# Second layer norm and weight splits moved into the first cycle of a delta-rule layer, with key norm and inverse turns re-placed between its scores

## The chip, the cores and the metric

The kernel runs on one core of a Trainium2 chip. The metric is the device time of one execution in microseconds (us). Engines: PE is TensorE (PEld its weight loads), DVE VectorE, ACT ScalarE, POOL GpSimd, SP the queue that issues the DMAs here. Each takes its own instructions in order and waits on semaphores.

## The reference

A small vision model of two blocks on 64 images of 38 tokens (2432 tokens of width D = 256): patch embedding, softmax attention, a mixture of experts, then the block that matters here, and a feed-forward layer with ternary weights. That block's attention, for 16 heads of 16:

```python
h = h + L1_attn(_layernorm(h))          # the "second layer norm" and the "delta layer"
# inside L1_attn
q = silu(x @ Wq); k = l2norm(silu(x @ Wk)); v = silu(x @ Wv)
log_f = log_sigmoid(x @ Wf); gamma = -sigmoid(x @ Wgamma)
a = k * gamma[..., None] * exp(gk)      # gk = log_f, per head
# per token: Sp = S * exp(gk); u = a.Sp + v; S = Sp + k u; o = q.S
out = out * sigmoid(x @ Wg1 @ Wg2)
out = layernorm(out) * norm_w
return out @ Wo
```

## The kernel before

Products run in float32r: each operand is split into a high part (ScalarE copies and rounds) and a low part (the difference), and three products are summed (`split_products`). XH and XL hold the normalised, transposed activations in these two parts, in 19 tiles of 128 tokens; the delta layer takes them in 8 chunks of 304 tokens (8 images).

**Stage of the second layer norm** (`layer_norm_turn`, called from `last_layer`), closed by a barrier of all engines (line 70) on both sides. DVE normalises a tile of the residual into one of four buffers `normed_tiles` (L138), PE transposes it with two matmuls into one of four PSUM banks (L169), ACT copies it to `x_hi` (L151), DVE writes `x_lo` (L128). SP loads the weights meanwhile, in 22 transfers (L105). Before tile 9 DVE waits for all of them and then prepares some weights (L1321 to L1326); ACT and POOL split five weights (L160, L115).

**Delta layer** (`delta_layer`): a pipeline over the 8 chunks in one function `part(c, nxt, z, y)` for each engine, whose calls are cycles k = 0, 1, ... 9. In cycle k, `nxt` = k is projected to queries and keys, `c` = k-1 gets its values, decays and scores, `z` = k-2 has the inverse of its 19x19 triangular systems computed row by row on DVE (`inverse_row`, L2367 multiplies and L2370 sums), and `y` = k-3 yields outputs. Cycle 0 has only `nxt` and the low-rank gate (`low_part` on PE, L2045; `low_high` on ACT, L2248; `gate_parts` on DVE, L2470); cycles 3 to 7 have all four. The order inside a cycle is the order of calls at the end of `part`, written by hand.

The end of a cycle on PE: `output` (L2141), then scores in four rounds (`score(p)`, L2034, all into the same four PSUM banks), decays (L2011), the transposed inverse in three batches of its rows (`inverse_out`, L2078, batches in `T_BATCHES`), then the next cycle's `a_rows` (L2055, L2061) and values (L1998). `score(p)` waits until DVE has weighed round p-1 (`weigh`, L2430). DVE between these: `whole_out` (L2451), `low_out` (L2459), `inverse_row(17)` and `(18)`, `bounded` (L2411) and `unit_key` (L2417). `key_norm` (L1982) sums the squares of the keys for `bounded`. POOL makes the next decay operands (`steps`, L2567), each after the decay matmul two before it.

Of the kernel before, what the change touches and what calls it, by code (L numbers as in the profile page):

```python
# [25 lines left out]
P = 128  # L26
# [57 lines left out]


def layer_norm_turn(nc, bank, RES, STD, MV, XN, XH, XL, ident, name, loads=(), splits=(),
                    prepare=None, pool_first=None, pool_work=None):

    xh = XH[:, :, 0:TOKENS]
    xl = XL[:, :, 0:TOKENS]
    first = TILES - len(splits) - 5
    with stage(nc, name + "_var", name + "_std", name + "_inv", name + "_normed", name + "_turned",
               name + "_hi", name + "_lo", name + "_loaded", name + "_prepared",
               name + "_w_hi", name + "_w_lo") as (
            block, var_ready, std_ready, inv_ready, normed, turned, hi_ready, lo_ready,
            loaded, prepared, w_hi, w_lo):  # L100
        if loads:
            @block.sync
            def _(sp):
                for dst, src in loads:
                    sp.dma_start(dst, src).then_inc(loaded, 16)  # L105
                sp.wait_ge(loaded, 16 * len(loads))

        if splits or pool_work:
            @block.gpsimd
            def _(pool):  # L110
                if pool_first:
                    pool_first(w_lo)
                for n, (raw, hi, lo) in enumerate(splits):
                    pool.wait_ge(w_hi, n + 1)
                    nc.gpsimd.tensor_tensor(lo, raw, hi.bitcast(F32), ALU.subtract).then_inc(w_lo, 1)  # L115
                if pool_work:
                    pool_work(pool, w_lo)

        @block.vector
        def _(dve):  # L120
            nc.vector.tensor_scalar(STD[:, 0, :], MV[:, :, 1], EPS, None, ALU.add).then_inc(var_ready, 1)
            dve.wait_ge(std_ready, 1)
            nc.vector.reciprocal(STD[:, 2, :], STD[:, 1, :]).then_inc(inv_ready, 1)
            dve.wait_ge(inv_ready, 1)

            def low_part(t):
                dve.wait_ge(hi_ready, t + 1)
                nc.vector.tensor_tensor(  # L128
                    xl[:, :, t * P:(t + 1) * P], bank[t % 4][:, 0:D].rearrange("p (m t) -> p m t", m=HALVES),
                    xh[:, :, t * P:(t + 1) * P].bitcast(F32), ALU.subtract).then_inc(lo_ready, 1)  # L130

            for t in range(TILES):
                if prepare and t == first - 1:
                    dve.wait_ge(loaded, 16 * len(loads))
                    prepare[0](prepared)
                if t >= 4:
                    dve.wait_ge(turned, t - 3)
                nc.vector.tensor_scalar(XN[:, t % 4, :], RES[:, t, :], MV[:, t, 0:1], STD[:, 2, t:t + 1],  # L138
                                        ALU.subtract, ALU.mult).then_inc(normed, 1)
                if t >= 2:  # L140
                    low_part(t - 2)
            low_part(TILES - 2)
            low_part(TILES - 1)

        @block.scalar
        def _(act):
            act.wait_ge(var_ready, 1)
            nc.scalar.activation(STD[:, 1, :], STD[:, 0, :], ACT.Sqrt).then_inc(std_ready, 1)
            for t in range(TILES):
                act.wait_ge(turned, t + 1)  # L150
                nc.scalar.activation(xh[:, :, t * P:(t + 1) * P],  # L151
                                     bank[t % 4][:, 0:D].rearrange("p (m t) -> p m t", m=HALVES),
                                     ACT.Copy).then_inc(hi_ready, 1)
                if t == first and splits:
                    act.wait_ge(loaded, 16 * len(loads))
                    if prepare:
                        act.wait_ge(prepared, prepare[1])
                if 0 <= t - first < len(splits):
                    raw, hi, lo = splits[t - first]
                    nc.scalar.activation(hi, raw, ACT.Copy).then_inc(w_hi, 1)  # L160

        @block.tensor
        def _(pe):
            for t in range(TILES):
                pe.wait_ge(normed, t + 1)
                if t >= 4:
                    pe.wait_ge(lo_ready, t - 3)
                for m in range(HALVES):
                    turn = nc.tensor.transpose(bank[t % 4][:, m * P:(m + 1) * P],  # L169
                                               XN[:, t % 4, m * P:(m + 1) * P], ident[:, :])  # L170
                turn.then_inc(turned, 1)
# [1114 lines left out]
def last_layer(nc, sb, psum, bank, ins, RES, BN, MV, STD, XN, XH, XL, xh_c, xl_c, ident, identb, hmask, out):  # L1286
# [9 lines left out]
    with ExitStack() as ctx:  # L1296
# [17 lines left out]
        with ExitStack() as raw:  # L1314
# [4 lines left out]
            def norm_into_output(scaled):  # L1319
                for m in range(HALVES):  # L1320
                    nc.vector.tensor_scalar(w[:, 4, m, :], w[:, 4, m, :], nw[:, m:m + 1], None,  # L1321
                                            ALU.mult).then_inc(scaled, 1)
# [1466 lines left out]
```

## Time and profile before

| what | value |
|---|---|
| median of 3 runs | 1803.45 us (1800.07 to 1805.45) |
| profiled execution, its own time | 1798.41 us |
| its span, first to last instruction | 1796.6 us |
| granted TensorE clock, mean | 0.89 |
| busy: PE, PEld, DVE, ACT, POOL | 1644.3, 1473.5, 1102.7, 682.4, 333.2 us |
| second layer norm (window of the trace) | 1172.85 to 1196.12 us |
| cycle 0 of the delta layer | 1196.74 to 1212.68 us |
| cycles 1 to 9 | 1212.68 to 1624.4 us |

Busy shares are means over stages with different limits: most of PE's time is the mixture of experts, up to 1172 us, which the change doesn't touch. Each stage is to be read from its own windows and from the wait that ends last in it.

### The profile page before, as it was taken

To read this page: it belongs to the slowest core of one execution; us is meant where nothing else is said; L and a number is where in the kernel's file an instruction comes from. 1 tells how busy PE (TensorE), PEld (TensorE's weight loads), DVE (VectorE), ACT (ScalarE), POOL (GpSimd) and SP (SyncE) were. 2 spreads that over 40 slices of the span, in tenths; PEclk is the share of its full clock that TensorE was granted. 3 is DMA by queue.
4 is the path that set the end of the run, shared out by engine and by line. 5 is a ranking of instruction groups with operands and counts; after the bars stand their busy time and mean duration, and the time that the engine had idled before them with its cause. 6 is when DMAs were issued, how large, how long until landed. Compare 5 with 4: busy or idle time off the path is not lost. (4 is left out here: it accounts for less than half of the span.)

```text
span 1796.6 us, 49076 instructions
## 1 busy us (share of the span) xinstructions
PE 1644.3 (92%) x21601; PEld 1473.5 (82%) x21601; DVE 1102.7 (61%) x2417; ACT 682.4 (38%) x1433; POOL 333.2 (19%) x331
## 2 busy tenths in 40 slices
PE   8899968999999999999999999967889889778789
PEld 8788856898888999999999999936888778767668
DVE  7677757555455554645555455565666675665885
ACT  6466644232122232322222232245343444324642
POOL 4633336000000000000000000044232222210840
PEclk9999969999999999999999999968676665665889
DMA  6000011000000000100001000010000000001001
GB/s 216 1 2 3 3 50 48 1 25 24 1 24 24 25 24 1 48 1 24 24 3 46 1 1 1 1 38 2 3 3 4 4 4 3 4 4 53 1 12 45
DMA packets 11702, 36.10 MB, mean 20 GB/s; under 512 B 3401, under 2 KB 8033, under 8 KB 8929
## 3 DMA queue, kind: packets, MB, share of 16 engines
q1 hardware_dynamic: 11488, 32.97, 5.3%
q8 instruction: 170, 2.79, 0.6%
q14 instruction: 44, 0.35, 0.1%
HBM read 30.47 MB, written 2.49 MB: 18 GB/s over the span
## 5 line engine op out<-in xcount | busy, mean ns | idle before, releaser
L1126 ACT ACTIVATE hidden<-bank,moe_b 128x512 f32<-128x512 f32 (+1 forms) x320 | 213.3, 668 | 536.8 <-PE bank L1018 522.5
L1035 PE MATMUL bank<-moe_w2h,hidden_hi 128*128 128x256 f32 x1216 | 345.7, 284 | 0.0
L1035 PE MATMUL bank<-moe_w2l,hidden_hi 128*128 128x256 f32 x1216 | 344.0, 283 | 0.0
L1035 PE MATMUL bank<-moe_w2h,hidden_lo 128*128 128x256 f32 x1216 | 343.9, 283 | 0.0
L1160 DVE SCALAR_TENSOR_TENSOR residual<-bank,gates,residual 128x256 f32<-128x256 f32 x152 | 73.4, 483 | 290.5 <-PE bank L1035 290.5
L1018 PE MATMUL bank<-x_hi,moe_w1h 128*128 128x512 f32 (+1 forms) x640 | 243.8, 381 | 2.9 <-ACT hidden L1126 2.8
L1018 PE MATMUL bank<-x_lo,moe_w1h 128*128 128x512 f32 (+1 forms) x640 | 242.5, 379 | 0.0
L1018 PE MATMUL bank<-x_hi,moe_w1l 128*128 128x512 f32 (+1 forms) x640 | 242.1, 378 | 0.0
L1035 PEld LDWEIGHTS bank<-moe_w2h,hidden_hi 128*128 128x128 f32 x1216 | 233.0, 192 | 5.9 <-DVE residual L1160 4.3
L1035 PEld LDWEIGHTS bank<-moe_w2l,hidden_hi 128*128 128x128 f32 x1216 | 233.2, 192 | 1.2
L1035 PEld LDWEIGHTS bank<-moe_w2h,hidden_lo 128*128 128x128 f32 x1216 | 233.2, 192 | 0.0
L1148 DVE TENSOR_TENSOR hidden_lo<-hidden,hidden_hi 128x512 fp32r<-128x512 f32 (+1 forms) x320 | 215.2, 672 | 11.0
L1146 DVE CAST hidden_hi<-hidden 128x512 fp32r<-128x512 f32 (+1 forms) x320 | 133.1, 416 | 87.1 <-ACT hidden L1126 79.5
L1335 POOL MEMSET gate_low<- 80x2432 f32 x1 | 2.1, 2121 | 867.0 <-POOLq L70 867.0
L1018 PEld LDWEIGHTS bank<-x_hi,moe_w1h 128*128 128x128 f32 x640 | 120.2, 188 | 25.9 <-ACT hidden L1126 5.0
L1018 PEld LDWEIGHTS bank<-x_hi,moe_w1l 128*128 128x128 f32 x640 | 120.1, 188 | 20.4
L1018 PEld LDWEIGHTS bank<-x_lo,moe_w1h 128*128 128x128 f32 x640 | 120.3, 188 | 18.7
L2567 POOL TENSOR_TENSOR decay_steps<-log_f_parts,from_here 128x608 fp32r<-128x608 f32 x64 | 78.9, 1244 | 212.4 <-PE bank L2011 126.9
L2367 DVE TENSOR_TENSOR normed_tiles<-a_rows,inverse 128x2 f32<-128x2 f32 (+5 forms) x144 | 68.9, 479 | 3.4
L2370 DVE TENSOR_REDUCE inverse<-normed_tiles 128x2 f32<-128x2 f32 (+5 forms) x144 | 57.4, 399 | 5.0
L2034 PE MATMUL bank<-q_and_k,dk_in_pair 32*64 32x76 f32 x2048 | 35.8, 275 | 25.1 <-DVE qk_and_ak L2430 24.6
L2430 DVE TENSOR_TENSOR qk_and_ak<-bank,decay 128x304 f32<-128x304 f32 x128 | 51.5, 463 | 10.2 <-PE bank L2034 5.4
(331 smaller groups left out, 3231.2 us busy)
## 6 DMA issues: line engine op xcount, KB each, us to landing
moe_w<-in_moe_w SPq DMA_DIRECT2D x16, 1024.0 KB, 4.8
patches<-in_patches SPq DMA_DIRECT2D x7, 864.0 KB, 6.6
out<-residual SPq DMA_DIRECT2D x19, 128.0 KB, 1.7
ffn_w<-in_ffn_w SPq DMA_DIRECT2D x2, 1024.0 KB, 6.3
att_w<-in_att_w SPq DMA_DIRECT2D x1, 1536.0 KB, 9.7
delta_w<-in_delta_w SPq DMA_DIRECT2D x1, 1280.0 KB
patches<-in_patches SPq DMA_DIRECT2D x6, 144.0 KB, 2.6
tok_w<-in_tok_w SPq DMA_DIRECT2D x6, 128.0 KB, 2.4
```

The source lines that it names most:

```text
L1018: mm = nc.tensor.matmul(bank[i % 4][:, 0:n], left, right, start=(j == 0), stop=(j == len(passes) - 1))
L1035: mm = nc.tensor.matmul(bank[4 + n % 3][:, 0:D], left, right, start=(i == 0), stop=(i == len(passes) - 1))
L1126: nc.scalar.activation(H[:, i % 4, 0:n], bank[i % 4][:, 0:n], ACT.Relu, bias=b1[:, x, f:f + 1]).then_inc(acted, 1)
L1146: nc.vector.tensor_copy(HH[:, k % 2, f, 0:n], H[:, i % 4, 0:n]).then_inc(h_hi, 1)
L1148: nc.vector.tensor_tensor(HL[:, k % 2, f, 0:n], H[:, i % 4, 0:n], HH[:, k % 2, f, 0:n].bitcast(F32), ALU.subtract).then_inc(h_lo, 1)
L1160: nc.vector.scalar_tensor_tensor(out=RES[:, t, :], in0=bank[4 + n % 3][:, 0:D], scalar=G[:, t, x:x + 1], in1=RES[:, t, :], op0=ALU.mult, o ...
L1335: nc.gpsimd.memset(G1[:].bitcast(F32), 0.0).then_inc(done, 1)
L2034: mm = nc.tensor.matmul(psum[half(s), g, ts], KX[rows, m, 2 * p + s, e, :], buffers["QK"][c % 2][rows, m, 2 * p + s].rearrange("p x t -> p ...
L2367: nc.vector.tensor_tensor(PD[:, :, 0:t, 0:t], spread(AS[:, :, t, 0:t], 2, t), TT[:, :, 0:t, 0:t], ALU.mult).then_inc(t_mult, 1)
L2370: nc.vector.tensor_reduce(TT[:, :, 0:t, t], PD[:, :, 0:t, 0:t], AX.X, ALU.add).then_inc(t_solved, 1)
L2430: nc.vector.tensor_tensor(PA[c % 2][:, p, m * HPH:(m + 1) * HPH].rearrange("p (g e) x t -> p e g x t", e=2)[:, e], psum[:, 0:PPH, n * 2 * ...
L2567: nc.gpsimd.tensor_tensor(MS[:, b % 2], spread(LF[:, :, b // 2, heads].bitcast(F32), 3, SEQ), spread(spread(here[:, :], 1, HPH), 1, 2), AL ...
```

## The change

The stage `layer_norm_turn` is gone. Its work becomes the `first` branch of `part` in cycle 0, interleaved with the projections, and its raw weights lie in the buffer `qk_and_ak1`, which the first cycles leave unused. The weights of Q and K are loaded by a transfer of their own, the others by 22 more. The normalisation is now `x * inv + (-mean * inv)`: even tiles on DVE, odd tiles on ACT. The low-rank product alternates between two banks. The memsets of POOL move behind the computed statistics. One `ACT_TABLE_LOAD` and one barrier fall away. Separately, in every cycle: `decay(3)` goes ahead of `score(0)`, `key_norm(1)` from before `decay(2)` to before `score(2)`, `inverse_row(17)` ahead of the first `weigh`, `inverse_row(18)` behind the third round's; the batches of inverse rows are 8, 3 and 8 where they were 8, 8 and 3.

```diff
-T_BATCHES = (range(0, 8), range(8, 16), range(16, HALF))
+T_BATCHES = (range(0, 8), range(8, 11), range(11, HALF))
 # PE, cycle 0 (project waits for x_lo of 3 tiles and for its weights' low part)
+                if first:
+                    turns(*range(8))
+                    project(0)
+                    turns(8, 9)
+                    project(1)
+                    turns(10, 11)
+                    low_part(0)
+                    project(2)
+                    turns(12, 13)
+                    low_part(1)
+                    project(3)
+                    turns(14, 15)
+                    low_part(2)
+                    turns(16, 17, 18)
+                    key_norm(0)
+                    low_part(3)
+                    key_norm(1)
+                    low_part(4)
+                    return
 # PE, every cycle, from output on
                 output(1)
-                key_norm(1)
                 decay(2)
+                decay(3)
                 score(0)
-                decay(3)
                 inverse_out(0)
                 score(1)
                 decay(4)
                 decay(5)
+                key_norm(1)
                 score(2)
                 decay(6)
                 decay(7)
+                inverse_out(1)
                 score(3)
-                inverse_out(1)
                 inverse_out(2)
 # DVE, cycle 0, its start
+                    norm(0)
+                    norm(2)
+                    low(0)
+                    for t in (4, 6, 8):
+                        norm(t)
+                        low(t - 3, t - 2)
+                    prepare()                  # waits for all 22 transfers
+                    silu_of(0)
+                    norm(10)
+                    low(7, 8)
...
+                    low(15, 16, 17, 18)
+                    bounded(0)
+                    gate_part(2)
+                    bounded(1)
+                    decay_masks()
+                    unit_key(0)
+                    unit_key(1)
+                    gate_part(3)
+                    gate_part(4)
+                    gate_weights()
 # POOL, cycle 0
+                    pool.wait_ge(inv_ready, 2)
                     nc.gpsimd.memset(after[:].bitcast(F32), 0.0).then_inc(zeroed, 1)
...
+                    low(0)                     # low part of the K weights, then of Q
+                    low(1)
+                    nc.gpsimd.memset(G1[:].bitcast(F32), 0.0).then_inc(gate_zero, 1)
+                    nc.gpsimd.memset(wg2s[:].bitcast(F32), 0.0).then_inc(gate_zero, 1)
+                    low(2)
+                    square(0)
+                    low(3)
+                    square(1)
```

On ScalarE, the first stretch before, from the start of the layer norm's stage (`std` is the standard deviation, `x_hi` the high part, `delta_wgh` and the next ones the high parts of weights):

```order
L148 ACT_TABLE_LOAD
L148 ACTIVATE std<-std 128x19
L151 ACTIVATE x_hi<-bank 128x2x128 x10
L160 ACTIVATE delta_wgh<-delta_wg_90 128x32
L151 ACTIVATE x_hi<-bank 128x2x128
L160 ACTIVATE delta_wvfh<-delta_wvf 128x576
L151 ACTIVATE x_hi<-bank 128x2x128
L160 ACTIVATE delta_wh<-delta_w 128x512
```

And on ScalarE in cycle 0 of the change (`normed_tiles` are the odd tiles, `sig_qk` the sigmoid of a projection):

```order
L2274 ACT_TABLE_LOAD
L2274 ACTIVATE std<-std 128x19
L2196 ACTIVATE normed_tiles<-residual,std 128x256 x2
L2202 ACTIVATE x_hi<-bank 128x2x128 x2
L2196 ACTIVATE normed_tiles<-residual,std 128x256
L2202 ACTIVATE x_hi<-bank 128x2x128 x2
L2196 ACTIVATE normed_tiles<-residual,std 128x256
L2202 ACTIVATE x_hi<-bank 128x2x128 x2
L2211 ACTIVATE delta_wh<-qk_and_ak_88 128x512 x2
L2196 ACTIVATE normed_tiles<-residual,std 128x256
L2202 ACTIVATE x_hi<-bank 128x2x128 x2
L2284 ACT_TABLE_LOAD
```

ACT got nine normalisations and does its weight splits earlier, between the tiles.

On TensorE, the end of cycle 3 before, from `output` to the next `a_rows`:

```order
L2141 MATMUL bank<-qk_and_ak_97 32x76 x64
L1982 MATMUL bank<-k_square_then_norm,same_head 128x304
L2011 MATMUL bank<-decay_steps,after 128x304 x2
L2034 MATMUL bank<-q_and_k_100,dk_in_pair 64x76 x32
L2011 MATMUL bank<-decay_steps,after 128x304 x2
L2078 MATMUL bank<-ident,inverse 64x64 x16
L2034 MATMUL bank<-q_and_k_100,dk_in_pair 64x76 x32
L2011 MATMUL bank<-decay_steps,after 128x304 x4
L2034 MATMUL bank<-q_and_k_100,dk_in_pair 64x76 x32
L2011 MATMUL bank<-decay_steps,after 128x304 x4
L2034 MATMUL bank<-q_and_k_100,dk_in_pair 64x76 x32
L2078 MATMUL bank<-ident,inverse 64x64 x22
```

And the same place of the change:

```order
L2076 MATMUL bank<-qk_and_ak_94 32x76 x64
L1931 MATMUL bank<-decay_steps,after 128x304 x4
L1954 MATMUL bank<-q_and_k_97,dk_in_pair 64x76 x32
L2013 MATMUL bank<-ident,inverse 64x64 x16
L1954 MATMUL bank<-q_and_k_97,dk_in_pair 64x76 x32
L1931 MATMUL bank<-decay_steps,after 128x304 x4
L1901 MATMUL bank<-k_square_then_norm,same_head 128x304
L1954 MATMUL bank<-q_and_k_97,dk_in_pair 64x76 x32
L1931 MATMUL bank<-decay_steps,after 128x304 x4
L2013 MATMUL bank<-ident,inverse 64x64 x6
L1954 MATMUL bank<-q_and_k_97,dk_in_pair 64x76 x32
L2013 MATMUL bank<-ident,inverse 64x64 x16
```

Behind the fourth score now stand 16 matmuls of the inverse where 22 stood, and they need the last row, where before 16 of the 22 did not.

On VectorE at that place before (`out_whole` is `whole_out`, `x_lo` is `low_out`, `qk_and_ak` is `weigh`, the 17x17 and 648 products are rows 17 and 18):

```order
L2451 SCALAR_TENSOR_TENSOR out_whole<-bank,in_pair,out_whole 128x152 x4
L2411 TENSOR_SCALAR k_square_then_norm<-bank 128x304
L2459 TENSOR_TENSOR x_lo<-out_whole,x_hi 128x2x2x38 x4
L2430 TENSOR_TENSOR qk_and_ak_97<-bank,decay 128x4x76 x4
L2367 TENSOR_TENSOR normed_tiles<-a_rows,inverse 128x2x17x17
L2370 TENSOR_REDUCE inverse<-normed_tiles 128x2x17
L2430 TENSOR_TENSOR qk_and_ak_97<-bank,decay 128x4x76 x4
L2367 TENSOR_TENSOR normed_tiles<-a_rows,inverse 128x648
L2370 TENSOR_REDUCE inverse<-normed_tiles 128x2x18
L2430 TENSOR_TENSOR qk_and_ak_97<-bank,decay 128x4x76 x4
```

And of the change:

```order
L2459 SCALAR_TENSOR_TENSOR out_whole<-bank,in_pair,out_whole 128x152 x4
L2375 TENSOR_TENSOR normed_tiles<-a_rows,inverse 128x2x17x17
L2378 TENSOR_REDUCE inverse<-normed_tiles 128x2x17
L2438 TENSOR_TENSOR qk_and_ak_94<-bank,decay 128x4x76 x4
L2467 TENSOR_TENSOR x_lo<-out_whole,x_hi 128x2x2x38 x4
L2438 TENSOR_TENSOR qk_and_ak_94<-bank,decay 128x4x76 x4
L2419 TENSOR_SCALAR k_square_then_norm<-bank 128x304
L2438 TENSOR_TENSOR qk_and_ak_94<-bank,decay 128x4x76 x4
L2375 TENSOR_TENSOR normed_tiles<-a_rows,inverse 128x648
L2378 TENSOR_REDUCE inverse<-normed_tiles 128x2x18
L2438 TENSOR_TENSOR qk_and_ak_94<-bank,decay 128x4x76 x4
```

Row 17 moved ahead of the first round, row 18 behind the third, `low_out` behind the first.

## Rows read from the trace of the kernel before

**Rows 1.** Windows by stage: length, busy us and instructions, granted clock, DMA share.

```profile
1172.85:1196.12 23.27, 12.22 (x38) 5.75 (x38) 18.63 (x45) 10.72 (x26) 7.89 (x7) 0.53 0.22 74
1196.74:1212.68 15.94, 13.44 (x58) 7.70 (x59) 10.68 (x18) 9.20 (x16) 10.38 (x17) 0.84 0.00 0
1276.48:1328.25 51.77, 47.09 (x1450) 42.32 (x1448) 34.62 (x82) 21.33 (x53) 13.63 (x15) 0.70 0.02 4
```

**Rows 2.** Timeline of the start: start us, us, engine, line, idle before.

```profile
1172.85 2.12 POOL L1335 MEMSET gate_low<- 80x2432 f32 x1 [866.96 <-POOLq L70]
1172.89 2.11 DVE L121 TENSOR_SCALAR std<-mean_var 128x19 f32<-128x19 f32 x1 [0.67 <-PEq L70]
1175.60 1.06 DVE L138 TENSOR_SCALAR normed_tiles<-residual,mean_var,std 128x256 f32<-128x256 f32 x3
```

**Rows 3.** Groups from 1172.8 to 1212.7: busy us, mean ns, idle before.

```profile
L151 ACT ACTIVATE x_hi<-bank 128x256 fp32r<-128x256 f32 x19 | 7.3, 384 | 11.2 <-PE bank L169 11.1
L2248 ACT ACTIVATE gate_low<-bank 16x512 fp32r<-16x512 f32 x4 | 2.0, 570 | 0.0
L160 ACT ACTIVATE delta_wh<-delta_w 128x512 fp32r<-128x512 f32 x3 | 1.9, 639 | 0.0
L148 ACT ACT_TABLE_LOAD x1 | 1.3, 1283 | 21.9 <-PEq L70 21.9
L138 DVE TENSOR_SCALAR normed_tiles<-residual,mean_var,std 128x256 f32<-128x256 f32 x19 | 9.9, 532 | 0.0
L128 DVE TENSOR_TENSOR x_lo<-bank,x_hi 128x256 fp32r<-128x256 f32 x19 | 7.9, 416 | 1.1 <-ACT x_hi L151 1.0
L169 PE MATMUL bank<-ident,normed_tiles 128*128 128x128 f32 x38 | 12.2, 445 | 12.5 <-DVE normed_tiles L138 12.5
```

**Rows 4.** Timeline: the wait for transfers, and a normalisation beside POOL.

```profile
1184.10 0.61 DVE L1321 TENSOR_SCALAR delta_w<-delta_w,norm_w 128x256 f32<-128x256 f32 x2 [3.20 <-DMA free_row<-in_from_here]
1189.84 3.86 POOL L115 TENSOR_TENSOR delta_wl<-delta_w,delta_wh 128x512 fp32r<-128x512 f32 x3
1190.28 1.03 DVE L138 TENSOR_SCALAR normed_tiles<-residual,mean_var,std 128x256 f32<-128x256 f32 x1
```

**Rows 5.** Timeline of cycle 0: one gate matmul at either clock.

```profile
1198.02 0.63 PE L2045 MATMUL bank<-x_hi,delta_wgh 128*16 128x512 f32 x1
1203.52 0.39 PE L2045 MATMUL bank<-x_hi,delta_wgh 128*16 128x512 f32 x1
```

**Rows 6.** Waits from 1260 to 1600 (total us, times, longest); PE's timeline, end of cycle 3.

```profile
PE bank L2034 <- DVE qk_and_ak L2430: 21.3, 17, 2.4
...
1320.25 0.95 PE L2034 MATMUL bank<-q_and_k,dk_in_pair 32*64 32x76 f32 x64 [1.18 <-DVE qk_and_ak L2430]
1324.37 1.24 PE L2034 MATMUL bank<-q_and_k,dk_in_pair 32*64 32x76 f32 x64 [2.42 <-DVE qk_and_ak L2430]
1325.54 2.79 PE L2078 MATMUL bank<-ident,inverse 64*64 64x64 f32 x44
```

**Rows 7.** Timeline of DVE and POOL there; last two from cycles 8 and 9.

```profile
1313.68 2.00 DVE L2459 TENSOR_TENSOR x_lo<-out_whole,x_hi 128x152 fp32r<-128x152 f32 x4
1315.61 1.60 DVE L2430 TENSOR_TENSOR qk_and_ak<-bank,decay 128x304 f32<-128x304 f32 x4
1320.11 1.82 DVE L2367 TENSOR_TENSOR normed_tiles<-a_rows,inverse 128x648 f32<-128x648 f32 x1
1579.86 0.83 DVE L2367 TENSOR_TENSOR normed_tiles<-a_rows,inverse 128x648 f32<-128x648 f32 x1
1617.88 0.99 DVE L2459 TENSOR_TENSOR x_lo<-out_whole,x_hi 128x152 fp32r<-128x152 f32 x4
```

**Rows 8.** Timeline, end of cycle 9.

```profile
1620.82 1.18 ACT L2256 ACTIVATE inverse_t<-bank 128x512 f32<-128x512 f32 x1 [0.69 <-PE bank L2078]
1622.11 0.97 PE L2078 MATMUL bank<-ident,inverse 64*64 64x64 f32 x12 [1.34 <-DVE inverse L2370]
1623.13 0.55 ACT L2256 ACTIVATE inverse_t<-bank 128x192 f32<-128x192 f32 x1 [1.12 <-PE bank L2078]
```

More of the change, by code:

```diff
@@ L83, in split_products @@
     return ((hi_l, hi_r), (hi_l, lo_r), (lo_l, hi_r))
[L86 to L171, printed above, removed]
@@ new lines, in last_layer @@
+        blocks = [(slice(HB * r, HB * r + HALF), slice(PAD * (r // 2) + HALF * (r % 2),
+                                                       PAD * (r // 2) + HALF * (r % 2) + HALF)) for r in range(4)]
+        free = [(slice(HB * r + HALF, HB * (r + 1)), slice((HB - HALF) * r + 1, (HB - HALF) * (r + 1) + 1))
+                for r in range(4)]
+        loads = ([(wg, ins["delta_wg1"]), (wvf[:, :, 0:D + HEADS], ins["delta_wvf"]), (w[:, 2:5], ins["delta_w"][:, 2:5]),
+                  (nw[:], ins["norm_w"]), (same[:], ins["same_head"]), (wg2[:], ins["delta_wg2"])]
+                 + [(here[dst, :], ins["from_here"][src, :]) for dst, src in blocks]
+                 + [(here[dst, :], ins["after"][src, 0:SEQ]) for dst, src in free]
+                 + [(free_row[dst, 0:2], ins["from_here"][SEQ:SEQ + HALF, SEQ - 2:SEQ]) for dst, src in blocks]
+                 + [(free_row[dst, 0:2], ins["from_here"][0:HB - HALF, SEQ - 2:SEQ]) for dst, src in free])
@@ L1884, in delta_buffers, with delta_layer @@
     }
[L1887 removed]
+def delta_layer(nc, psum, bank, buffers, stages, first_load, loads):
     Q, K, O = range(3)
@@ L2299, in high_out @@
                     nc.scalar.activation(out_view(xh_c, y, j, s), OW[:, j, s], ACT.Copy).then_inc(o_hi, 1)
+                if first:
+                    act.wait_ge(var_ready, 1)
+                    nc.scalar.activation(STD[:, 1, :], STD[:, 0, :], ACT.Sqrt).then_inc(std_ready, 1)
+                    norm(1)
+                    for t in (3, 5, 7):
+                        norm(t)
+                        high(t - 3, t - 2)
+                    split(0)
+                    split(1)
+                    norm(9)
+                    high(6, 7)
+                    nc.scalar.preload_act_table_set("sigmoid_and_others")
+                    sigmoid(0)
+                    norm(11)
+                    high(8, 9)
+                    split(2)
+                    sigmoid(1)
+                    norm(13)
+                    high(10, 11)
+                    split(3)
+                    low_high(0)
+                    norm(15)
+                    high(12, 13)
+                    sigmoid(2)
+                    padded(0)
+                    low_high(1)
+                    norm(17)
+                    high(14, 15)
+                    sigmoid(3)
+                    padded(1)
+                    high(16, 17, 18)
+                    split(4)
+                    low_high(2)
+                    nc.scalar.preload_act_table_set("natural_log_exp_and_others")
+                    inverse_norms()
+                    low_high(3)
+                    low_high(4)
+                    return
                 nc.scalar.preload_act_table_set("natural_log_exp_and_others")
@@ L2317, in part @@
                 sigmoid(3)
-                for i in range(len(spans)):
-                    low_high(i)
                 nc.scalar.preload_act_table_set("natural_log_exp_and_others")
@@ L2604, in part @@
                         pool.wait_ge(g1_again, i + 1)
+                    return
+                for m in range(HALVES):
+                    for e in range(2):
+                        keys_in_pair(m, e)
+                steps(0)
+                steps(1)
+                square(0)
+                square(1)
                 for b in range(2, CB):
```

215 lines of the change are left out of this document (137 added, 78 removed).

## The prediction

> **What bounds the kernel now.** I read the windows by stage first. The stage of the layer norm lasts 23.27 us and cycle 0 behind it 15.94 us; with the barrier between them they end at 1212.68, 39.83 us after 1172.85, when cycle 1's values start on PE [rows 1]. In the first of the two no engine is full: DVE has 18.63 us of work, PE 12.22, ACT 10.72, POOL 7.89, and the clock was granted at 0.53, so nearly all at 1.2 GHz [rows 1]. In cycle 0 PE has 13.44 of 15.94 us, ACT 9.20 and DVE 10.68. So two stages, one bound by DVE and one by PE, stand one behind the other.
>
> The grouped work says what the DVE-bound stage consists of: 19 normalisations at a mean of 532 ns and 19 low parts at 416 ns; ACT's 19 high parts are 384 ns and it idles 11.1 us for PE [rows 3]. The timeline adds two waits: at the start the first DVE instruction takes 2.11 us beside a POOL memset of 2.12, so that the first normalisation starts only at 1175.60, 2.75 us in [rows 2]; and before tile 9 DVE idles 3.20 us for the last of the 22 transfers, until 1184.10, 11.25 us in [rows 4].
>
> Then the end of the cycles. Cycles 3 to 7 are full ones of the length of cycle 3, 51.77 us with 47.09 of PE busy [rows 1]. From the wait table, PE waits for DVE's weighing 21.3 us in 17 waits between 1260 and 1600 [rows 6]; in cycle 3 the two are 1.18 and 2.42 us, ahead of the third and fourth score [rows 6]. That is the only repeated wait there that ends on another engine's work, 3.6 us a cycle.
>
> **The change, first cycle.** Time counts from the stage's start, now 0. I walk the queues with row durations.
>
> Start: POOL now waits for the statistics, so the first DVE instruction loses its 2.11 us. ACT's table load is 1.28 and ends the wait instead; its root, DVE's reciprocal and the new product of mean and inverse are small instructions of 0.2 to 0.3 us. First normalisation at about 2.1, where it was 2.75: 0.65 gained. POOL's memsets then run beside the first tiles and hold one DVE normalisation back, up to 2 us; PE has the ACT tile meanwhile. I take 1 us lost there.
>
> Tiles: DVE starts three normalisations in 1.06 us, so one each 0.33 [rows 2], and a low part each 0.32 to 0.42 [rows 3]. Before, DVE paid both for each tile, 0.65 us; now it pays half of the normalisations, about 0.49. ACT pays per pair two high parts and one normalisation, three times 0.3 to 0.38, so 0.45 to 0.57. Neither lies far below the 0.65 before, and turning a tile costs PE two matmuls of 445 ns that overlap, 0.47. With first weights split by ACT behind tile 5 and by POOL in 1.29 us each (3.86 for three [rows 4]), PE can start project(0) at 8.8.
>
> The transfers: one more is issued, so they are complete at about 11.25 + 0.5 = 11.7. DVE reaches `prepare` at 9.2 and stalls there again; queued behind it are silu_of(0), normalisation 10 and low parts 7 and 8. PE is covered for most of that: from 8.8 it has two projections (1.5 each at 1.2 GHz: 304 columns are 0.25, times six) and turns 8 and 9, until 12.8. It then waits for normalisation 10, until 13.5.
>
> From there PE has five gate products, two projections, nine turns, two key norms. A gate product is six matmuls of 512 columns, each 0.43 at 1.2 GHz and 0.21 to 0.23 at 2.4 (rows of 0.63 and 0.39 with the same tail [rows 5]), so 2.6 or 1.4. At 2.4 GHz this is 7.0 (5 x 1.4) + 1.7 + 4.0 + 0.8 = 13.5, so 27.0; my walk, with handoffs partly hidden, has the last gate product end at 26.1. Behind it: ACT has its table load and four norms of the keys before low_high(3) and (4), ending at 28.2, DVE's last two gate parts 29.2, and values start at **29.3**. ACT as a whole has 19 x 0.3 to 0.38, 9 normalisations, three splits of 0.64, five gate copies of 0.57, three table loads of 1.28 [rows 3] and some 6 us more, about 25; so it alone would allow 26. Gain: 39.8 - 29.3 = **10.5 us**.
>
> Bounds. Best: nothing waits beyond ACT's own 26, gain 14. Worst: PE stays at 1.2 GHz, then from 8.8 it has 6.1 (four projections) + 5.2 (11 turns) + 12.8 + 1.4 = 25.5, so 34.3, plus 3.1 of tail, gain 2.5. I keep 10.5: cycle 0 before was granted 0.84 in the mean [rows 1], 1.2 GHz in its first gate products and 2.4 GHz once PE had worked on them without a gap, and such a stretch begins here at 8.8.
>
> DVE's ten normalisations cost 1.03 beside POOL's splits where they cost 0.40 alone [rows 2, 4]; with POOL's work of some 19 us inside the same cycle I count 4 of them so, 2.5 us, inside the walk. The row of the start (2.11 beside 2.12) shows DVE held for the whole memset. The Trainium skill, "SBUF — State Buffer", section "Who interferes with whom", says the pair of ports that VectorE shares with GpSimd is an exclusive lock for a whole instruction, and lists tensor_scalar (our normalisation), and tensor_tensor with two SBUF inputs against a GpSimd read. The trace agrees on both. By that rule all of POOL's queue could fall on DVE's ten: ten times 0.63 is 6.3 us instead of 2.5, and the gain 6.7.
>
> **The change, end of a cycle.** Taken at cycle 3. Row 17 now follows `whole_out` on DVE, where `low_out` stood from 1313.68 on, and meets POOL's decay operand; row 18 shows the price: 1.82 us beside POOL, 0.83 without [rows 7]. So row 17 ends at 1315.5 and the first weighing starts where it did, 1315.61 [rows 7]. What changes is what follows. `low_out` no longer meets POOL: 0.99 for four instead of 2.00 [rows 7]. A round is 1.60 [rows 7], the next instruction 1.53 behind its start: 1315.6 + 1.5 + 1.0 + 1.5, so the second ends at 1319.7. The third score (0.95 [rows 6]) starts at 1319.8 instead of 1320.25; its weighing no longer has row 18 ahead of it, 2.6 us with its wait for POOL, and starts at 1320.8 where it started at 1322.7 (1320.11 + 1.82 + 0.8 for the sum). The fourth score starts at 1322.4, before at 1324.37. Row 18 then runs 1.7 us, to 1324.1, and the last batch of the inverse waits for it: 32 passes, 2.79 x 32/44 = 2.03 [rows 6], so PE is free at 1326.2 instead of 1328.25. What was late (the fourth score) is followed by row 18: **2.0 us** gained, out of 3.6 waited.
>
> If PE is at 1.2 GHz in the rounds (scores of 1.24 and more [rows 6]) the same walk gives 1.2. If POOL gets ahead of row 17 twice, another 1.2 goes: bounds 0 and 3.6. I take 1.7, five times (cycles 3 to 7): 8.5.
>
> The other cycles. Cycle 1 has no inverse; decay(3) ahead of the first score costs 0.3. In cycle 2 row 17 delays the first weighing by 1.5 while no output hid it: 0.3 lost. Cycle 8, 0.4 gained. Cycle 9 has no scores to hide anything: behind row 18 stood 12 passes in 0.97 and a copy of 0.55, now 32 passes in 2.03 and a copy of 1.18 [rows 8]: 1.1 + 0.6 = 1.7 lost for certain, since the next stage starts behind it.
>
> **Sum.** 10.5 + 8.5 - 0.3 - 0.3 + 0.4 - 1.7 = 17.1 us. Against the profiled execution's own 1798.41 (span 1796.6 and 1.8 around it) this is 1781.3; the median of the runs lies 5.0 above that execution, so the forecast is 1803.45 - 17.1 = **1786.4**.
>
> **The rivals.**
> 1. *The reordering gives nothing* (0.18). Row 17 and POOL's operands collide, and the weighing starts 1.2 later. For it: 1.82 against 0.83 [rows 7], and POOL's next two operands follow each other there. Against it: row 18 leaves the path either way. 10.5 - 1.9 = 8.6: 1794.8.
> 2. *The first cycle stays at 1.2 GHz, or POOL holds DVE* (0.10). For it: 0.53 granted in the stage whose turns now fill half of PE's queue [rows 1]. Against it: project and gate products are the kind of stretch in which it rose. Gain 2.5 to 6.7 + 6.6: 1790 to 1794.
> 3. *Slower* (0.04). The clock in the cycles: the key norm, a product over the whole array, no longer stands ahead of the scores. Cycle 3 had 0.70 [rows 1], so 40% of it, 21 us, at 2.4 GHz. All at 1.2 GHz, with scores going from 0.95 to 1.24, would add 0.3 x 21 = 6.3 a cycle, 31 in five: 1817. It decides the sign when it costs over 3.4 a cycle. Against it: waits leave PE, and less idling stands before the scores, not more.
>
> The likeliest (0.68) is both gains, 1786.4, its own range 1779 to 1792.
>
> **Numbers.** A measurement of this kernel tells 0.3% from no change, 5.4 us: faster means below 1798.0. Rivals 1 and 2 remain below it at their centres, with some tail above: faster 0.91, same 0.05, slower 0.04. The range 1775 to 1797 takes in both rivals' centres; its low end lies just above both best bounds together (14 + 5 x 3.6 - 1.9 = 30.1: 1773.3).
>
> **What would show it.** After: values of cycle 1 start 27 to 32 us after the stage's start; DVE waits once for DMA, about 2.5 us; PEclk high from the middle of cycle 0. Cycles 3 to 7 last 49 to 51 us; the wait ahead of the fourth score is below 1 us and a new wait of PE for `inverse` appears ahead of the last batch. Cycle 9 is 1.7 longer. Wrong would be: a granted clock in the cycles below 0.6, a gap of PE behind project(1) of over 3 us, or the multiplications of row 17 at 2 us or more.

## The result, and the profile after

The changed kernel took 1788.31 us in the median of 4 runs (1785.84 to 1788.63) against 1803.55 of the kernel before on the same chip: ratio 0.9915, interval 0.9897 to 0.9932, 15.2 us less. A second pair of medians from another chip (run `changed_again` below) gave 0.9926 (0.9913 to 0.9938), 13.3 us less. The forecast was 17.1 us less. The profiled execution took 1788.13 us, 10.3 less than that of before, since the latter lay 5 us below its own median. Its granted clock was 0.899 in the mean, where 0.89 was granted before.

The windows by stage, on the changed kernel: first cycle with the layer norm in it, cycle 1, cycle 3, cycle 9 (length, then busy us of PE, PEld, DVE, ACT, POOL, granted clock, DMA share, GB/s):

```profile
1174.56:1207.72 33.16, 20.81 (x97) 13.47 (x97) 27.16 (x58) 25.10 (x55) 19.68 (x26) 0.84 0.17 52
1207.72:1235.16 27.44, 20.24 (x325) 17.02 (x325) 12.34 (x32) 14.13 (x37) 12.39 (x13) 0.75 0.01 2
1276.47:1325.26 48.79, 46.77 (x1450) 41.65 (x1448) 33.49 (x83) 21.36 (x52) 14.11 (x14) 0.72 0.02 4
1573.39:1613.68 40.29, 26.48 (x1126) 25.09 (x1125) 20.12 (x50) 12.38 (x19) 0.00 (x0) 0.53 0.02 4
```

The first line stands against both stages of [rows 1] and the barrier between them: 33.2 us instead of 39.8, 6.6 gained. The third stands against cycle 3 there: 48.79 instead of 51.77. The second is the surprise: cycle 1 had been 23.28 and is 27.44, and its granted clock is 0.75 where it had been 1.00. The window of cycle 1 in the kernel before:

```profile
1212.68:1235.96 23.28, 15.37 (x324) 12.75 (x324) 14.37 (x36) 16.36 (x42) 15.20 (x17) 1.00 0.01 2
```

The timeline of the end of cycle 0 in the changed kernel shows what stood ahead of the values (start, us, engine, line; idle time before it in brackets):

```profile
1192.02 3.33 DVE L2474 TENSOR_SCALAR normed_tiles<-residual,std 128x256 f32<-128x256 f32 x1
1192.29 1.13 POOL L2664 MEMSET inverse<- 128x1216 f32 x1
1193.38 1.82 POOL L2666 MEMSET dk_in_pair<- 128x2048 f32 x1
1195.41 0.83 PE L1964 MATMUL bank<-ident,normed_tiles 128*128 128x128 f32 x4 [1.29 <-DVE normed_tiles L2474]
1203.53 0.94 ACT L2218 ACTIVATE gate_low<-bank 16x512 fp32r<-16x512 f32 x2
1204.58 0.64 DVE L2522 TENSOR_SCALAR from_here<-from_here,free_row 128x38 f32<-128x38 f32 x1
1205.13 1.15 DVE L2425 TENSOR_TENSOR q_and_k<-q_and_k,k_square_then_norm 128x304 f32<-128x304 f32 x2
1206.31 1.15 DVE L2502 TENSOR_TENSOR gate_low<-bank,gate_low 16x512 fp32r<-16x512 f32 x2
1207.72 0.58 PE L1918 MATMUL bank<-delta_wvfh,dchunk_hi 128*128 128x288 f32 x1 [4.83 <-DVE gate_low L2502]
1208.09 0.44 PE L1918 MATMUL bank<-delta_wvfl,dchunk_hi 128*128 128x288 f32 x1
```

Two things are to be read from it. Normalisation 14 took 3.33 us beside GpSimd's memsets, eight times its 0.40 alone. And ACT had copied the last gate rows at 1204.5, but DVE worked through decay masks and unit keys before it took them up at 1206.31; PE waited 4.83 us. The first 12 of its next 24 products last 0.44 us or more (0.58 the first), the last 11 of them 0.29, as nearly all 24 do in the kernel before.

PE's waits from 1250 to 1590 in the changed kernel (total us, times, longest) stand against the first row of [rows 6]:

```profile
PE bank L1954 <- DVE qk_and_ak L2438: 8.1, 12, 2.2
PE bank L2013 <- DVE inverse L2378: 4.3, 7, 0.7
```

and its timeline of DVE and then PE at the end of cycle 3 against the rest of it and [rows 7]:

```profile
1312.21 1.64 DVE L2375 TENSOR_TENSOR normed_tiles<-a_rows,inverse 128x578 f32<-128x578 f32 x1
1314.56 1.60 DVE L2438 TENSOR_TENSOR qk_and_ak<-bank,decay 128x304 f32<-128x304 f32 x4
1316.08 0.98 DVE L2467 TENSOR_TENSOR x_lo<-out_whole,x_hi 128x152 fp32r<-128x152 f32 x4
1321.50 0.82 DVE L2375 TENSOR_TENSOR normed_tiles<-a_rows,inverse 128x648 f32<-128x648 f32 x1
...
1318.93 0.95 PE L1954 MATMUL bank<-q_and_k,dk_in_pair 32*64 32x76 f32 x64 [0.50 <-DVE qk_and_ak L2438]
1321.64 0.95 PE L1954 MATMUL bank<-q_and_k,dk_in_pair 32*64 32x76 f32 x64
1323.24 2.09 PE L2013 MATMUL bank<-ident,inverse 64*64 64x64 f32 x32 [0.65 <-DVE inverse L2378]
```

The wait for the weighing fell from 21.3 to 8.1 us; the fourth score no longer waits (it had waited 2.42); a short wait for row 18 is new. Row 17 (form 128x578) meets GpSimd and takes 1.64; `low_out` and row 18 (128x648) no longer do. That is the walk of the prediction, row for row.

### The profile page after: what moved, and what is told of

It reads as the page before. It is cut to its first block and busy times, and to the rows that moved or that the text cites. A ratio compares the mean times of both kernels' runs of the same rounds, so it can differ in the third digit from the quotient of the medians.

```text
span 1786.3 us, 49082 instructions
## 1 busy us (share of the span) xinstructions
PE 1641.7 (92%) x21601; PEld 1474.8 (83%) x21601; DVE 1092.3 (61%) x2409; ACT 685.3 (38%) x1441; POOL 335.3 (19%) x331
## 5 line engine op out<-in xcount | busy, mean ns | idle before, releaser
L930 PEld LDWEIGHTS bank<-x_hi,moe_w1l 128*128 128x128 f32 x640 | 120.2, 188 | 20.4
L930 PEld LDWEIGHTS bank<-x_lo,moe_w1h 128*128 128x128 f32 x640 | 120.3, 188 | 18.6
L2378 DVE TENSOR_REDUCE inverse<-normed_tiles 128x2 f32<-128x2 f32 (+5 forms) x144 | 57.4, 399 | 4.9
L824 POOL TENSOR_TENSOR probs<-probs,row_inv 128x608 f32<-128x608 f32 x32 | 38.7, 1211 | 91.7 <-DVE row_inv L714 91.7
```

The lines of the kernel that those rows point to most:

```text
L824: nc.gpsimd.tensor_tensor(PR[:, n % 2, :, 0:SEQ], PR[:, n % 2, :, 0:SEQ], spread(RI[:, n % 2, :], 2, SEQ), ALU.mult).then_inc(normed, 1)
L930: mm = nc.tensor.matmul(bank[i % 4][:, 0:n], left, right, start=(j == 0), stop=(j == len(passes) - 1))
L2378: nc.vector.tensor_reduce(TT[:, :, 0:t, t], PD[:, :, 0:t, 0:t], AX.X, ALU.add).then_inc(t_solved, 1)
```

## The experiments

Twelve runs, one of them the changed kernel again, each timed beside the kernel before on its own chip; runs of different chips are compared by their ratios. The table reads their profiled executions, one of each. "Start" is from the first DVE instruction of the stage to the first value product of cycle 1; "gap" is PE's idle time ahead of it; "product" is the median length of the 24 products behind it; "cycle 1" has its granted clock in brackets; "tail, 3 to 7" is the sum over cycles 3 to 7 of the time from the start of the last row of `whole_out` on DVE to the next cycle's `a_rows` on PE, split at the first weighing. All times in us.

| kernel | ratio (95%) | start | gap | product | cycle 1 | tail, 3 to 7 | cycle 9 |
|---|---|---|---|---|---|---|---|
| before | 1 | 39.8 | 2.46 | 0.29 | 23.3 (1.00) | 17.5 + 63.0 | 37.7 |
| changed | 0.9915 (0.9897, 0.9932) | 33.2 | 4.83 | 0.40 | 27.4 (0.75) | 14.7 + 53.5 | 40.3 |
| changed_again | 0.9926 (0.9913, 0.9938) | 33.2 | 4.83 | 0.45 | 26.0 (0.87) | 14.7 + 53.5 | 38.6 |
| first_cycle_only | 0.9972 (0.9960, 0.9984) | 33.2 | 4.84 | 0.44 | 25.2 (0.84) | 20.4 + 63.3 | 38.4 |
| orders_only | 0.9960 (0.9947, 0.9974) | 39.7 | 2.47 | 0.43 | 27.5 (0.75) | 14.3 + 53.9 | 39.7 |
| row17_alone | 0.9959 (0.9946, 0.9972) | 39.0 | 2.46 | 0.29 | 23.3 (1.00) | 16.0 + 57.4 | 37.1 |
| row18_alone | 0.9968 (0.9956, 0.9980) | 38.3 | 2.47 | 0.44 | 25.4 (0.80) | 18.4 + 58.2 | 37.8 |
| key_norm_alone | 1.0002 (0.9992, 1.0012) | 38.4 | 2.46 | 0.29 | 26.4 (0.79) | 16.4 + 63.2 | 38.1 |
| gates_first | 0.9906 (0.9890, 0.9922) | 29.7 | 1.35 | 0.29 | 24.5 (0.91) | 14.2 + 54.8 | 40.4 |
| memsets_late | 0.9916 (0.9901, 0.9931) | 31.1 | 5.26 | 0.44 | 26.6 (0.82) | 14.4 + 53.7 | 39.6 |
| batches_back | 0.9908 (0.9894, 0.9922) | 33.2 | 4.84 | 0.44 | 26.0 (0.87) | 14.3 + 54.1 | 36.8 |
| gates_batches | 0.9877 (0.9863, 0.9891) | 29.9 | 1.35 | 0.29 | 26.3 (0.80) | 13.9 + 54.6 | 37.3 |
| gates_c1 | 0.9875 (0.9860, 0.9890) | 29.9 | 1.35 | 0.29 | 23.9 (0.90) | 14.3 + 54.1 | 37.7 |
| gates_memsets | 0.9879 (0.9865, 0.9893) | 29.1 | 1.35 | 0.29 | 25.5 (0.87) | 14.7 + 54.4 | 37.8 |

Single executions differ also in what an edit leaves as it was. In the five kernels with the layer norm of before, "start" is 38.3 to 39.8; with the same orders the whole tail is 80.5 in the kernel before and 83.7 in `first_cycle_only`, whose `low_out` met GpSimd for longer; cycle 1 of the changed kernel is 27.4 and 26.0. A difference of 1 to 3 us in one column, from one execution, is no result by itself.

**The two halves of the change.** `first_cycle_only` is the changed kernel with the cycles' orders and batches of before; `orders_only` is the kernel before with the new ones:

```diff
 # first_cycle_only, against the changed kernel (PE and ACT likewise as before)
+T_BATCHES = (range(0, 8), range(8, 16), range(16, HALF))
+                bounded(1)
                 low_out ...
                 weigh(0); weigh(1)
+                inverse_row(17)
```

> The moved layer norm alone: cycles as before. Before 1803.5, changed kernel 1788.3. Forecast of the prediction: 10.5 us less than before, 1793. My theory after the two traces: 6.6 us less up to the values of cycle 1, and 1.4 given back in cycle 1, whose value products start at 1.2 GHz behind a gap of PE: 5.2 us less than before, 1798.3, with cycle 1 at 24.7 us. Rival: the whole 4.2 us by which cycle 1 grew belong to this part: 2.4 us less, 1801.1, cycle 1 at 27.4 us.

> The three orders and the batches of the inverse in the kernel before, layer norm as before. Forecast of the prediction: 6.6 us less than before, 1796.9. My theory after the traces: cycles 3 to 7 together 12.8 less, cycle 8 0.6 less, cycle 1 2.8 more, cycle 2 0.8 more, cycle 9 2.6 more: 7.2 less, 1796.3. Rival: cycle 1 grows only behind the new first cycle: 10 us less, 1793.5.

The moved layer norm is worth 5.0 us (1800.96 x 0.0028; interval 2.9 to 7.2), the orders 7.2 (4.7 to 9.5). Together 12.2, which is at the very low end of the interval of the whole on the first chip (12.3 to 18.6) and inside that of the second (11.1 to 15.6). Both came out where the theory from the traces put them; the forecast's 10.5 for the first half lies outside its interval, its 6.6 for the second inside.

**The end of cycle 0.** `gates_first` lets the gate copies and gate parts pass what stood ahead of them, `memsets_late` moves the memsets off normalisation 14:

```diff
 # gates_first, ACT
                     low_high(2)
+                    low_high(3)
+                    low_high(4)
                     nc.scalar.preload_act_table_set("natural_log_exp_and_others")
                     inverse_norms()
-                    low_high(3)
-                    low_high(4)
 # gates_first, DVE
                     bounded(1)
+                    gate_part(3)
+                    gate_part(4)
                     decay_masks()
                     unit_key(0)
                     unit_key(1)
-                    gate_part(3)
-                    gate_part(4)
 # memsets_late, POOL
                     square(1)
+                    pool.wait_ge(normed_even, 10)
                     nc.gpsimd.memset(TT[:, :, :, :], 0.0).then_inc(zeroed, 1)
```

> Changed kernel with the last two gate copies of ACT ahead of its table load and the keys' norms, and DVE's last two gate parts ahead of the decay masks and the unit keys. Theory: the 4.83 us gap of PE ahead of the values falls to about 1.4, and the clock is not lost in it, so the values run at 2.4 GHz: 3.4 + 1.4 less than the changed kernel, 1783.5. Rival: the unit keys come later, and with them POOL's keys and the first score; what is gained ahead of the values is lost ahead of the scores: 1788.

> Changed kernel with POOL's three memsets of inverse, inverse_t and dk_in_pair held until DVE's last normalisation is done. Theory (a normalisation can't run while POOL works through memsets): normalisation 14 takes 0.40 instead of 3.33 us, PE's wait of 1.29 for it goes, and the values start 1.3 to 2.9 us earlier: 1786.2. Rival (the end of cycle 0 hangs on ACT's norms of the keys and DVE's masks, which start when PE's key products are done): no change, 1788.3.

In `gates_first` the timeline of PE shows the gap at 1.35 us and the first product at 0.37:

```profile
1204.61 0.37 PE L1918 MATMUL bank<-delta_wvfh,dchunk_hi 128*128 128x288 f32 x1 [1.35 <-DVE gate_low L2502]
```

Values start 3.5 us earlier (29.7 instead of 33.2), and cycle 1 has lost none of it. The time is 0.9906 where the changed kernel had 0.9915 and 0.9926: 1.6 to 3.6 us less, each less than the two intervals together can tell; `gates_batches` below settles it only together with the other edit. `memsets_late` shows, in its timelines of DVE and PE:

```profile
1192.28 0.47 DVE L2474 TENSOR_SCALAR normed_tiles<-residual,std 128x256 f32<-128x256 f32 x1
...
1205.88 0.58 PE L1918 MATMUL bank<-delta_wvfh,dchunk_hi 128*128 128x288 f32 x1 [5.26 <-DVE gate_low L2502]
```

The normalisation takes 0.47 instead of 3.33, so the memsets were its cause, and values start 2.1 us earlier. The time, 0.9916, doesn't show them: 1 to 2 us are below what the runs tell. Part of them was also given back at once: the gap ahead of the values is 5.26 here, 23 of the 24 products behind it last 0.44 or so where 12 did, and the 24 take 6.0 us instead of 4.8.

**The orders, one by one.** The changed kernel was run again as their measure, and three edits were made alone, in the kernel before; `batches_back` is in the changed one:

```diff
 # row17_alone, DVE
                 bounded(1)
+                inverse_row(17)
+                weigh(0); weigh(1)
                 low_out ...
-                weigh(0); weigh(1)
-                inverse_row(17)
 # row18_alone, DVE
-                inverse_row(18)
                 weigh(4); weigh(5)
+                inverse_row(18)
 # key_norm_alone: PE (DVE: bounded(1) behind weigh(3), unit keys last; ACT: inverse_norms behind the decays)
-                key_norm(1)
                 decay(2)
+                decay(3)
                 score(0)
-                decay(3)
                 ...
+                key_norm(1)
                 score(2)
 # batches_back
+T_BATCHES = (range(0, 8), range(8, 16), range(16, HALF))
```

> The changed kernel itself once more, unedited, as the measure for the others on this chip and for how far cycles of one kernel differ between two executions. Both theories: 0.9915 of the kernel before; values of cycle 1 start 33.2 us after the stage's start, cycles 3 to 7 together 248 us.

> Kernel before with one edit: row 17 of the inverse ahead of the first weighing, behind the second key bound. The prediction's walk: low_out no longer meets GpSimd, row 17 meets it instead, the first weighing starts when it did; third score 0.45 us earlier a cycle, so about 2 us less in cycles 3 to 7, 1799. Rival (row 17 lengthens what stands ahead of the first weighing by 1.2 us or more): 3 to 6 us more than before.

> Kernel before with one edit: row 18 of the inverse behind the sixth weighing. The prediction's walk: the fourth score's wait of 2.42 us goes, the last batch is only 12 passes and waits little: 2.0 us less in each of cycles 3 to 7, 10 us less than before, 1791. Rival (the weighing's place in DVE's queue gives nothing unless row 17 and the key bound move too): 2 to 3 us less in all, 1798.5.

> Kernel before with one edit: the second key norm between second and third score (with its bound on DVE behind the fourth weighing, its inverse on ACT behind the decays, and unit keys behind the last weighing) and decay(3) ahead of the first score; rows 17 and 18 and the batches as before. The prediction priced this at nothing in the full cycles. My theory: the bound no longer stands ahead of low_out and the first weighing, 0.9 us earlier a cycle, but low_out and row 18 still meet GpSimd: 3 to 4 us less than before, and cycle 1 1.2 us longer; 0.9985. Rival: that move is the source of the gain: 0.996 as with all orders.

> Changed kernel with the inverse's three batches at 8, 8 and 3 rows as before; the second batch, now 32 passes, still stands ahead of the fourth score. Theory: behind row 18 only 12 passes and a copy of 0.55 us are left, so cycle 9 loses its 1.7 us again and the 0.65 us wait for row 18 in each of cycles 3 to 8 shrinks: 1.7 to 5 us less than the changed kernel, 1785. Rival: the 32 passes hold the fourth score and its weighing up by 1 us a cycle, which nothing gives back: 3 us more, 1791.

`row17_alone` gives 7.4 us (5.0 to 9.7), as much as all orders together, where I had expected 2 and the rival a loss. What row 18, the key norm and the batches add to it is therefore not shown; a kernel with the new first cycle and this one move was not run. Its timeline of DVE and POOL at the end of cycle 3:

```profile
1314.32 0.75 DVE L2367 TENSOR_TENSOR normed_tiles<-a_rows,inverse 128x578 f32<-128x578 f32 x1
1315.78 1.61 DVE L2430 TENSOR_TENSOR qk_and_ak<-bank,decay 128x304 f32<-128x304 f32 x4
1317.30 0.98 DVE L2459 TENSOR_TENSOR x_lo<-out_whole,x_hi 128x152 fp32r<-128x152 f32 x4
1320.48 0.83 DVE L2367 TENSOR_TENSOR normed_tiles<-a_rows,inverse 128x648 f32<-128x648 f32 x1
...
1314.48 2.83 POOL L2567 TENSOR_TENSOR decay_steps<-log_f_parts,from_here 128x608 fp32r<-128x608 f32 x2 [2.95 <-PE bank L2011]
```

The one move takes `low_out` off GpSimd's operands and, since everything behind comes earlier, row 18 as well: 0.83 in place of 1.82. Row 17 itself started 0.16 us ahead of GpSimd's operand here and took 0.75; in cycles 4, 6 and 7 it took 1.5 to 1.8. I had priced only the neighbours that the edit names, not the row 18 that it shifts.

`row18_alone` gives 5.8 us (3.6 to 7.9); 10 were expected. Its tail is 4.8 us shorter behind the first weighing and 0.9 longer ahead of it: `low_out` still meets GpSimd (2.0 to 3.0 us), as in the kernel before. `key_norm_alone` gives nothing, 0.4 us more (1.4 less to 2.2 more), neither my 3 to 4 us less nor the rival's gain. Its tail shows why, in the timeline of DVE:

```profile
1314.47 2.60 DVE L2459 TENSOR_TENSOR x_lo<-out_whole,x_hi 128x152 fp32r<-128x152 f32 x4
1316.99 1.60 DVE L2430 TENSOR_TENSOR qk_and_ak<-bank,decay 128x304 f32<-128x304 f32 x4
1321.88 1.35 DVE L2367 TENSOR_TENSOR normed_tiles<-a_rows,inverse 128x648 f32<-128x648 f32 x1
```

With the bound gone from ahead of it, `low_out` starts at once, beside GpSimd, and takes 2.60; cycle 1 is 3.1 us longer. The prediction's nothing for this edit holds in the full cycles. In cycle 1 the trace doesn't settle it: the granted clock there was 0.79 instead of 1.00, and it fell at 1220.71, while PE's order differs from that of before only behind `decay(1)`, at 1223.27.

`batches_back` is 0.9908, against 0.9926 of the changed kernel on the same chip: 3.3 us less, with intervals that overlap. Its timeline of PE at the end of cycle 9 shows 12 passes behind row 18 where there were 32:

```profile
1604.00 0.92 PE L2013 MATMUL bank<-ident,inverse 64*64 64x64 f32 x12 [1.25 <-DVE inverse L2378]
1606.29 0.88 PE L1410 MATMUL bank<-values,inverse_t 32*19 32x16 f32 x43 [1.38 <-PEq L70]
```

Cycle 9 is 36.8 us instead of 38.6 and 40.3. The rival is out: 32 passes ahead of the fourth score lengthen the part behind the first weighing by 0.1 us a cycle (10.82 for 10.71), not by 1.

**Combinations.** `gates_batches` joins `gates_first` and `batches_back`; `gates_c1` adds cycle 1's old order on PE, `gates_memsets` the wait of `memsets_late`:

```diff
 # gates_c1, PE, against gates_batches
+                if c == 0:
+                    key_norm(1)
                 decay(2)
+                if c != 0:
+                    decay(3)
                 score(0)
+                if c == 0:
+                    decay(3)
```

> Changed kernel with the two edits gates_first and batches_back together. Theory (they lie in different cycles and add up): values start 29.7 us after the stage's start with products at 2.4 GHz, cycle 9 at about 37 us; 0.9888 of the kernel before (0.9926 less 0.0018 for each), 20 us less. Rival (gates_first was no gain beyond the scatter of its runs): 0.9908.

> gates_batches with one edit: in cycle 1 alone TensorE's second key norm stands ahead of the scores and decay(3) behind the first score, as in the kernel before. Theory: the new order costs cycle 1 1.2 us when its values run at 2.4 GHz (24.49 against 23.28), so cycle 1 lasts 23.3 us and the kernel 1.2 us less than gates_batches. Rival: the 1.2 us is scatter of the clock: no change.

> gates_batches with one edit: GpSimd's memsets of inverse, inverse_t and dk_in_pair held until DVE's last normalisation is done. Theory: normalisation 14 takes 0.4 us instead of 3.33, and now that the gate parts no longer stand behind the masks the 2 us arrive at the values: they start 27.6 us after the stage's start, 2 us less than gates_batches. Rival: the memsets now hold the masks and the split of the output weights up, the scores of cycle 1 come no earlier: no change.

`gates_batches` took 1778.01 us against 1800.27: 0.9877, 22.3 us less than before and clear of both intervals of the changed kernel, so the two edits together are worth 7 to 9 us. Against `batches_back` alone it is 5.6 us less (0.9877 and 0.9908; the intervals end at 0.9891 and begin at 0.9894, so they are just apart). `gates_first` by itself had shown 1.6 to 3.6, so it is worth some 2 to 6 us. It is the version that I would keep. `gates_c1` has the short cycle 1 again (23.9 for 26.3) and the same time (0.9875): 2 us are not told by these runs, and in its profiled execution other cycles were longer by as much. `gates_memsets` starts its values 0.8 us earlier and not 2, since normalisation 14 beside the memsets took only 2.14 us in `gates_batches`, not 3.33; no difference in time.

## Why the prediction was right, and where a term was off

**The end of the cycles: right.** The walk for cycle 3 had 10.6 us from the first weighing to the next cycle (1315.6 to 1326.2). Every one of cycles 3 to 7 took 10.7 in the changed kernel, in both executions, and 12.2 to 12.8 before. Row 17's collision was foreseen (1.82 priced, 1.64 measured), as was the new wait for row 18 (0.65). The tail is 12.3 us shorter in five cycles where 8.5 were taken: I had cut the 2.0 of the walk to 1.7 for a clock of 1.2 GHz that didn't come in the rounds, and cycle 3 was a mild model for cycles 5 and 6, in which `low_out` had taken 3.0 us beside GpSimd, not 2.0. Rival 1 (the reordering gives nothing) falls with `orders_only`. So does rival 3 for these cycles: the clock in the tails rose. (In cycle 1, for which I had not priced it, it fell from 1.00 to 0.75.) The windows from the last `whole_out` to the end of cycle 3 and of cycle 5, before:

```profile
1312.44:1328.25 15.81, 12.20 (x346) 10.41 (x344) 13.99 (x29) 6.43 (x17) 7.35 (x8) 0.83 0.02 4
1415.70:1432.40 16.70, 13.00 (x346) 10.99 (x344) 14.63 (x29) 6.27 (x16) 7.42 (x8) 0.70 0.01 3
```

and in the changed kernel:

```profile
1311.63:1325.26 13.63, 12.16 (x346) 10.21 (x344) 12.65 (x29) 6.26 (x17) 5.27 (x4) 0.94 0.02 4
1410.86:1424.53 13.67, 11.83 (x347) 10.07 (x345) 12.69 (x29) 6.26 (x17) 5.27 (x4) 0.95 0.01 4
```

The granted clock is 0.94 where it was 0.83, and 0.95 where it was 0.70. The gain doesn't hang on it: in the changed kernel cycles with 0.87 to 0.99 have tails of the same 13.63 to 13.68 us, in both executions. That the clock follows from the shorter waits is argued, not shown.

**The first cycle: the mechanism was right, the term 10.5 us was mis-sized.** It measured 5.0 with all that follows from it. That lies inside rival 2's bracket for this half (2.5 to 6.7), and half of that rival's reason came true: GpSimd held DVE, though the clock was granted at 0.84 and not at 1.2 GHz. Three steps of the working were off:
- "My walk has the last gate product end at 26.1": it ended at 28.3. PE's own work, as I had added it up, already gave 27.0, and the walk came out below it without a reason that holds. I had counted four normalisations at 1.03 us beside POOL's splits; none met those, but two at the start took 2.30 together beside memsets, and one took 3.33: 4.5 us held on the ten, where I had 2.5 and 1 at the start. `memsets_late` gives 2.1 us of this back.
- "DVE's last two gate parts 29.2": I had their input right (ACT's copies) and left out that the decay masks and unit keys stand ahead of them on DVE. The tail was 4.8 us, not 3.2. `gates_first` gives 3.5 back.
- Cycle 1 at + 0.3: it was + 4.2, and + 2.7 in the second execution. More of it goes with the clock than with the order. Over the fourteen executions the length goes with the granted clock: 23.3 us at 1.00 (twice), 23.9 and 24.5 at 0.90 and 0.91, 25.5 to 26.0 at 0.87, 25.2 to 26.6 between 0.79 and 0.84, 27.4 and 27.5 at 0.75. At nearly the same clock the new order is longer by 0.5 us (24.5 for 23.9) to 1.4 (26.6 at 0.82 for 25.2 at 0.84). The slow value products are 1.4 us of it (4.82 us for the 24 instead of 3.43). Whether the new order also lowers the clock is not shown; `gates_c1`, which puts the old one back in cycle 1, had 0.90 and 23.9 us where `gates_batches` had 0.80 and 26.3, in one execution each and without a difference in time.

My bounds for the gain were 2.5 to 14, and "the worst" was PE at 1.2 GHz; what happened was not that, but one normalisation held by a row of memsets, masks and keys ahead of the gate parts on DVE's queue, and a cycle 1 at a lower clock. Of the signs that I had named, the start of the values (27 to 32) was missed with 33.2; the single wait for transfers was 1.55 and not 2.5; cycles 3 to 7 lasted 48.4 to 51.8 and not quite the 49 to 51; the clock (high from 12.4 us on, 0.84 in the mean of the first cycle), the fourth score without a wait, the new wait for row 18 and cycle 9 (2.6 and 1.0 longer in two executions, 1.7 forecast) came as written. None of the three signs of being wrong appeared: PE's gap behind `project(1)` was 0.90 us, row 17 took 1.64 to 1.68.

The whole was nevertheless 15.2 for 17.1, and that is in part luck. In the two traces the terms are: 6.6 us gained up to the values and 4.2 lost in cycle 1, where I had 10.5 and 0.3; 12.8 gained in cycles 3 to 7, where I had 8.5; 0.8 lost in cycle 2, 0.6 gained in cycle 8, 2.6 lost in cycle 9. That is 12.4, so the stretch up to the end of cycle 1 fell short by 8 and cycles 3 to 7 made up 4 of it. Outside these cycles the changed kernel's trace is 2.1 us longer, 1.7 of it ahead of the first window, where nothing was changed, so the two profiled executions differ by 10.3. That the medians differ by 15.2 and not by 10.3 is no term of mine: the profiled execution of before lay 5 us below its median.

## What to carry to other kernels

When stages are merged, walk the queue behind each instruction that another engine waits for: what had been hidden in a later stage (masks, unit keys) now stands ahead of it, and here moving two gate copies and two gate parts ahead of what stood before them was worth some 2 to 6 us (5.6 in `gates_batches` against `batches_back`, 1.6 to 3.6 in `gates_first`). Moving one operation off a collision with GpSimd moves everything behind it too; look for the collisions of those, which may be the larger part (`row17_alone`). And a schedule made for the full cycles should be read once more in the cycles at either end, where nothing covers what it puts last.

## What the runs showed of the hardware

- **A row of memsets held one DVE instruction for the length of all three of them.** Normalisation 14 started at 1192.02 and ended at 1195.35, beside the end of a GpSimd square (1191.65 to 1192.35) and three memsets that ran from 1192.29 to 1195.20; it did not get in between them. With the memsets held back it took 0.47 beside the same square. A multiplication with two inputs in SBUF, by contrast, was held for only part of GpSimd's two operands (1.64 us beside 2.89), and for none of it where it started 0.16 us ahead. The Trainium skill, "SBUF — State Buffer", section "Who interferes with whom", says that whoever issues first has the shared ports for the whole instruction and that the other blocks. The multiplication agrees with that. The normalisation does not by its record, which begins 0.27 us ahead of the first memset, and a wait over three instructions of the other engine is more than the section says; no run here tells what let the memsets go first.
- **The clock behind a gap.** Of the 24 value products, 12 to 23 ran at the 1.2 GHz level (0.44 us each) in all five kernels whose gap ahead of them was 4.8 to 5.3 us, beginning with the first to the third of them. With a gap of 1.35 none did in four kernels (0.29 each, the 2.4 GHz level). Behind a gap of 2.46 it went either way with the same code ahead: none in three kernels, 13 in two, in one of these only from the twelfth product on. The Trainium skill, "TensorE: Matmul & The Clock Gate", part "HAM oscillation — how this bites in real kernels", tells of matmuls that fall back to the low clock behind a wait for a transfer; these runs agree for a wait for DVE, and show that a gap of the middle size decides it differently from run to run.
- **PE fully busy at 1.2 GHz.** A clock of 0.50 was granted to 12 us in the middle of full cycles with PE busy throughout, as in this window of cycle 3 in the kernel before:

```profile
1300.48:1312.48 12.00, 12.00 (x408) 10.15 (x402) 8.57 (x16) 4.89 (x10) 2.42 (x2) 0.50 0.02 4
```

The 12 us ahead of the last row of `whole_out` have 0.50 in each of cycles 3 to 7 of the changed kernel too, with PE busy for all 12.00 in four of them and for 11.07 in cycle 7. Its products are small tiles of 32 and 64 rows; no run here tells why the clock stays low.
